# Unread TensorE products placed where three stages of a graph network kernel meet

## The chip, the cores and the metric

The kernel runs on one core of a Trainium2 chip. It is one launch with three stages that follow each other. The metric is the device time of the launch in microseconds; lower is better. TensorE's clock has two levels, 1.2 and 2.4 GHz; the profile lists the granted clock as a share of the full one, so 0.50 is the lower level.

## The reference, cut to what matters

There are 128 graphs of 128 nodes with 512 features each. An attention layer with 16 heads and a bias from the adjacency matrix is followed by a residual and a layer norm; then each graph is sent to one of four experts, multiplied by that expert's weights and its adjacency, batch-normalised over all graphs of the same expert, and added and layer-normalised again.

```python
# attention, per graph: x is 128x512, adj 128x128
a = einsum('bhnd,bhmd->bhnm', q, k) * scale + (adj + adj)[:, None]
p = softmax(a)                       # rows that are all zero give 0
x = layernorm(x + einsum('bhnm,bhmd->bhnd', p, v) @ Wo.T)
# experts
top1 = argmax(x.mean(axis=1) @ router_w + router_b)
out  = adj @ (x @ expert_w[top1])
# batch norm over all graphs of one expert: sums of out and out*out per expert
mean, var = s / cnt, ss / cnt - mean * mean
x = layernorm(x + relu((out - mean[top1]) * rsqrt(var[top1] + eps) * gamma[top1] + beta[top1]))
```

## The kernel before, in words

**Attention stage.** It works on one graph per step, 128 steps, four unrolled; the last four steps (124 to 127) are written out behind the loop. Weights and activations are split into a high and a low part, and each product is made of three passes (high by high, high by low, low by high). In step t TensorE transposes the 16 heads' probabilities (four groups, `transposes(c)`, line 235), multiplies them by the values (`weighted_values`, L243), computes the scores of graph t+1 (`scores`, L197), values of graph t+2 (`v_parts`, L185) and four query or key units of graph t+3 (`qk_unit`, L176), and the output product of graph t (L293). The softmax of t+1 runs meanwhile: VectorE adds the bias and finds the maxima (L384), ScalarE takes exponentials (L316), GpSimd scales by the row sums (L519). VectorE and ScalarE copy the transposed probabilities out of PSUM (L434, L344). In the last three steps the work for later graphs is missing, so step 126 has no values or units to compute, and step 127 no scores either. VectorE adds the residual and normalises (L461 to L494), SyncE stores the result. A semaphore `qk_done[1]` counts the copies (VectorE) of the units that lie in the PSUM bank `BANK_A`.

**Expert stage.** All engines meet at the end of a stage. Then GpSimd clears the accumulators (L819, L820), ScalarE and VectorE split the four experts' weights into high and low parts (L720, L787), of which two are loaded in this stage, and TensorE computes `y = adj @ x` of the first two graphs (`y_product`, L658, f32 operands) and the router scores (L664). It then waits for the last weight split (`e_lo_done`) and enters the loop: per graph one `y_product` two graphs ahead and the product with the chosen expert's weights (`out_product`, L680). ScalarE copies it out and squares it, GpSimd adds both to the sums of the expert (L830, L834).

**Last stage.** TensorE sums the accumulators over the rows (L944, 16 instructions), transposes the sums (L950); VectorE and GpSimd compute mean, variance and the reciprocal root (L1018 to L1035, L1093); TensorE transposes the result (L954) and spreads it into rows (L964, L970), VectorE and ScalarE copy these (L1042, L1133). Then a loop over 128 tiles in a ring of 16: GpSimd multiplies a tile (L1104), TensorE adds the shift (L984, L985), VectorE adds the residual and takes statistics (L1053, L1058), GpSimd takes the reciprocal root for each four tiles (L1119), ScalarE normalises and stores. The loads of a tile wait for the ring slot's store.

Each engine takes its instructions in the order written; what ties them is semaphores.

Of the kernel before, what the change touches and what calls it, by code (L numbers as in the profile page):

```python
# [25 lines left out]
P = 128  # L26
# [18 lines left out]
def attention_phase(nc, io, W_hi, W_lo, w_stage, expert_w_in, ident, x1_dram, B, D):  # L45
    C = D // P
# [6 lines left out]
    Q, K, V, O = range(4)  # L53

    with ExitStack() as ctx:
# [32 lines left out]
        bank = [ctx.enter_context(nc.psum_tensor(f"att_bank{i}", [P, D], F32)) for i in range(8)]  # L88
# [24 lines left out]
        def for_steps(eng, body):  # L113

            with eng.Fori(0, LAST // UNROLL) as i:
                for s in range(UNROLL):
                    body(i * UNROLL + s, s, i, False)
            for s in range(UNROLL):
                body(LAST + s, s, LAST // UNROLL, True)
# [49 lines left out]
        @block.tensor  # L169
        def _(pe):  # L170
            def qk_unit(n, c, which, par, b):

                dst = bank[b][:, 0:GN]
                todo = [(w, x, k) for w, x in passes(W_hi, W_lo, xt_hi, xt_lo) for k in range(C)]
                for m, (w, x, k) in enumerate(todo):
                    mm = pe.matmul(dst, w[:, which, k, c * P:(c + 1) * P], x[:, par, k, :],  # L176
                                   start=m == 0, stop=m == len(todo) - 1)
                mm.then_inc(qk_ps, 1)

            def v_parts(s, b):  # L180

                par, j = (s // 2) % 2, s % 2
                todo = [(x, w, k) for x, w in passes(xt_hi, xt_lo, W_hi, W_lo) for k in range(C)]
                for m, (x, w, k) in enumerate(todo):
                    mm = pe.matmul(bank[b][:, :], x[:, par, k, j * P:(j + 1) * P], w[:, V, k, :],  # L185
                                   start=m == 0, stop=m == len(todo) - 1)
                    if m == len(todo) - 1:
                        mm.then_inc(v_ps, 1)
                    yield

            def scores(s):

                par, j = (s // 2) % 2, s % 2
                for c in range(C):
                    for r in range(HC):
                        rows = slice(r * HD, (r + 1) * HD)
                        mm = pe.matmul(bank[r][:, c * P:(c + 1) * P],  # L197
                                       qk[rows, par, Q, c, j * P:(j + 1) * P],
                                       qk[rows, par, K, c, j * P:(j + 1) * P], start=True, stop=True)
                mm.then_inc(s_ps, 1)  # L200

            for n in range(8):
                if n == 0:
                    pe.wait_ge(xt_lo_done, 1)
                if n % C == 0:
                    pe.wait_ge(w_lo_done, n // C + 1)
                if n >= 2:
                    pe.wait_ge(qk_done[n % 2], n // 2)  # L210
                qk_unit(n, n % C, n // C, 0, BANK_B - n % 2)
            for done in qk_done:
                pe.wait_ge(done, 4)
            scores(0)
            pe.wait_ge(w_lo_done, 3)
            for s in range(2):
                for _ in v_parts(s, BANK_B - s):
                    pass
            pe.wait_ge(xt_lo_done, 2)
            for n in range(8, AHEAD):  # L220
                if n < 10:
                    pe.wait_ge(v_done, n - 7)
                else:
                    pe.wait_ge(qk_done[n % 2], n // 2)
                qk_unit(n, n % C, Q, 1, BANK_B - n % 2)
            pe.wait_ge(const_done, 3)

            def body(t, s, i, last):


                def transposes(c):
                    pe.wait_ge(probs_done, 4 * t + c + 1)
                    for r in range(HC):
                        h = c * HC + r
                        mm = pe.transpose(bank[c][:, r * P:(r + 1) * P], probs[:, h * P:(h + 1) * P],  # L235
                                          ident[:, :])
                    mm.then_inc(pt_ps, 1)

                def weighted_values(c):
                    pe.wait_ge(pt_odd if c % 2 else pt_even, 2 * t + c // 2 + 1)  # L240
                    for r in range(HC):
                        h = c * HC + r
                        mm = pe.matmul(bank[BANK_O][r * HD:(r + 1) * HD, c * P:(c + 1) * P],  # L243
                                       v_sb[:, s, h * HD:(h + 1) * HD], probs_t[:, h * P:(h + 1) * P],
                                       start=True, stop=True)
                    if c == C - 1:
                        mm.then_inc(pv_ps, 1)

                def some_values(n):
                    for _ in range(n):  # L250
                        next(values, None)

                if exists(t, last, 2):
                    pe.wait_ge(res_done, t + 1)
                    values = v_parts((s + 2) % UNROLL, BANK_WO)
                else:
                    values = iter(())
                pe.wait_ge(v_done, t + 1)
                transposes(0)
                transposes(1)  # L260
                transposes(2)
                transposes(3)
                some_values(6)
                for c in range(C):
                    weighted_values(c)
                if exists(t, last, 1):


                    for done in qk_done:
                        pe.wait_ge(done, 2 * (t + 1 - (s + 1) % 2) + 4)  # L270
                    scores((s + 1) % UNROLL)
                some_values(6)

                def next_unit(k):

                    ahead = s + 3
                    if k == 0 and s % 2:
                        pe.wait_ge(xt_lo_done, i * 2 + ahead // 2 + 1)
                    pe.wait_ge(qk_done[k % 2], AHEAD // 2 + 2 * t + k // 2)
                    qk_unit(AHEAD + 4 * t + k, k, ahead % 2, (ahead // 2) % 2, BANK_B - k % 2)  # L280

                more_units = exists(t, last, 3)
                if more_units:
                    next_unit(0)
                pe.wait_ge(w_lo_done, 4)
                pe.wait_ge(o_lo_done, t + 1)
                if exists(t, last, 2):
                    pe.wait_ge(v_done, t + 3)
                else:
                    pe.wait_ge(res_done, t + 1)  # L290
                todo = [(a, w, k) for a, w in passes(o_hi, o_lo, W_hi, W_lo) for k in range(C)]
                for m, (a, w, k) in enumerate(todo):
                    mm = pe.matmul(bank[BANK_WO][:, :], a[:, k, :], w[:, O, k, :],  # L293
                                   start=m == 0, stop=m == len(todo) - 1)
                mm.then_inc(wo_ps, 1)
                if more_units:
                    for k in range(1, UNITS):
                        next_unit(k)

            for_steps(pe, body)  # L300

        @block.scalar
        def _(act):
# [237 lines left out]
def expert_phase(nc, io, W_hi, W_lo, w_stage, expert_w_in, ones, expert_row, kept, out_sum, out_sq,  # L541
# [4 lines left out]
    C = D // P  # L546
    HALF = C // 2
    ROUNDS = 2
    with ExitStack() as ctx:
# [51 lines left out]
        def for_steps(eng, body):  # L601


            def rounds(i, last):
                for n in range(ROUNDS):
                    for s in range(UNROLL):
                        r = i * ROUNDS + n
                        body(r * UNROLL + s, s, r, last, (n, s) == (ROUNDS - 1, UNROLL - 1))

            with eng.Fori(0, B // (ROUNDS * UNROLL) - 1) as i:  # L610
                rounds(i, False)
            rounds(B // (ROUNDS * UNROLL) - 1, True)
# [36 lines left out]
        def _(pe):  # L649
# [11 lines left out]
            def router_scores(pair):  # L661
                pe.wait_ge(part_done, 2 * pair + 2)
                pe.wait_ge(expert_done, pair + 1)
                pe.matmul(ps_scores[:, :, :].rearrange("p g e -> p (g e)"), ones[:, :],  # L664
                          part_score[:, :, :].rearrange("p g e -> p (g e)"),
                          start=True, stop=True).then_inc(scores_ps, 1)
# [19 lines left out]
            for s in range(2):  # L686
                y_product(s, s, 0)
            router_scores(0)
            pe.wait_ge(e_lo_done, E)

            loaded = []
# [16 lines left out]
                    loaded.append(load_expert(t + 1))  # L708

            for_steps(pe, body)  # L710

        @block.scalar
        def _(act):
# [125 lines left out]
def norm_phase(nc, io, ident, ones, expert_row, kept, out_sum, out_sq, x1_dram, y_dram, out_dram, B, D, E):  # L839

    C = D // P
# [6 lines left out]
    with ExitStack() as ctx:  # L848
# [89 lines left out]
        def _(pe):  # L938
# [10 lines left out]
            for c in range(C):  # L949
                mm = pe.transpose(ps_cols[:, c, :], sums_sb[:, c * P:(c + 1) * P], ident[0:2 * E, 0:2 * E])  # L950
            mm.then_inc(cols_ps, 1)

            pe.wait_ge(cols_done, 1)
            pe.transpose(ps_col_t, cols[:, :, :, :].rearrange("p a w n -> p (a w n)"),  # L954
# [262 lines left out]
```

## Time and profile before

| | |
|---|---|
| median of 3 runs | 2780.07 us (2777.33 to 2781.09) |
| the profiled execution's own time | 2777.71 us |
| its span, first to last instruction | 2776.0 us |
| mean granted TensorE clock | 0.985 |
| busy share PE, DVE, ACT, POOL | 96%, 69%, 54%, 46% |
| instructions | 77841 |

The span is the time between the first and the last instruction on any engine; the execution's time is a little longer. PE is TensorE, PEld its weight loads, DVE VectorE, ACT ScalarE, POOL GpSimd, SP SyncE. Busy shares are averages over three stages with different limits. The attention stage lasts until 1997 us, the expert stage until 2514.7 us, the last stage to the end. A row of a timeline gives the start, the duration, the engine, the line of the kernel, the operation, what it writes and reads, how many instructions were merged into the row, and in brackets how long the engine was idle before it and what ended that. Ends of products are modelled and include a tail in which the next one already runs.

### The profile page before, as it was taken

Reading aid. Unit: us, or ns where it says so; the run is one execution under the profiler, and the core shown is the slowest. Engines: PE = TensorE matmul, PEld = TensorE weight load, DVE = VectorE, ACT = ScalarE, POOL = GpSimd, SP = SyncE. Lnnn points to the kernel's source line nnn. Section 1 sums busy time; section 2 is a strip of 40 time slices with the busy share of each in tenths; the row PEclk is TensorE's granted clock in tenths of the full one; section 3 lists DMA queues with packets and bytes.
Section 4 is the critical chain, followed back from the end, with each engine's and each line's share of the span. In section 5 each row is a group of like instructions: output and inputs, shape, how many; then the busy total and the mean of one; then the engine's idle time right before and its main releaser. Section 6 shows DMA issues by size and latency. Waiting matters only on the chain. (4 is left out here: it accounts for less than half of the span.)

```text
span 2776.0 us, 77841 instructions
## 1 busy us (share of the span) xinstructions
PE 2660.1 (96%) x22583; PEld 2264.4 (82%) x22584; DVE 1921.5 (69%) x8351; ACT 1511.9 (54%) x5391; POOL 1282.4 (46%) x1174
## 2 busy tenths in 40 slices
PE   8999999999999999999999999999699999997776
PEld 7898989898888888898989898888588888883322
DVE  6777777777777777777777777777633333335887
ACT  5566665656565656565656656565534444442444
POOL 2343434333433343333334343333256666666887
PEclk9999999999999999999999999999799999998998
DMA  3111111111111111111111111111234444445999
GB/s 147 62 53 54 53 61 53 54 57 57 58 49 64 51 57 53 61 53 54 53 61 53 54 53 61 55 52 57 70 120 137 133 137 132 136 134 198 398 405 346
DMA packets 169427, 277.32 MB, mean 100 GB/s; under 512 B 19378, under 2 KB 52146, under 8 KB 168882
## 3 DMA queue, kind: packets, MB, share of 16 engines
q1 hardware_dynamic: 150962, 243.36, 26.2%
q10 hardware_dynamic: 18432, 33.56, 3.2%
q8 instruction: 15, 0.25, 0.0%
q14 instruction: 18, 0.15, 0.0%
HBM read 184.57 MB, written 92.27 MB: 100 GB/s over the span
## 5 line engine op out<-in xcount | busy, mean ns | idle before, releaser
L519 POOL TENSOR_TENSOR probs<-probs,row_scale 128x512 f32<-128x512 f32 x512 | 532.6, 1040 | 1107.6 <-DVE row_scale L408 1104.7
L316 ACT ACTIVATE probs<-neg_s,neg_max 128x128 f32<-128x128 f32 x2048 | 793.3, 392 | 138.1 <-DVE neg_max L384 138.1
L384 DVE CUSTOM_DVE_ANT_0 neg_s<-att_bank,adj_nat 128x128 f32<-128x128 f32 x2048 | 442.6, 286 | 3.8 <-PE att_bank L197 1.7
L316 ACT ACTIVATION_READ_ACCUMULATOR probs<-neg_s,neg_max 128x1 f32 x2048 | 390.6, 191 | 0.0
L393 DVE TENSOR_REDUCE abs_max<-neg_s 128x4 f32<-128x512 f32 x512 | 349.3, 682 | 0.1
L176 PE MATMUL att_bank<-xt_hi,att_w_hi 128*128 128x256 f32 x2048 | 329.3, 283 | 10.9 <-DVE att_w_lo L366 10.9
L176 PE MATMUL att_bank<-xt_hi,att_w_lo 128*128 128x256 f32 x2048 | 329.7, 283 | 0.0
L176 PE MATMUL att_bank<-xt_lo,att_w_hi 128*128 128x256 f32 x2048 | 329.1, 283 | 0.0
L176 PEld LDWEIGHTS att_bank<-xt_hi,att_w_hi 128*128 128x128 f32 x2048 | 298.8, 191 | 30.4 <-issue 10.5
L344 ACT ACTIVATE probs_t<-att_bank 128x512 f32<-128x512 f32 x256 | 152.9, 597 | 283.4 <-PE att_bank L235 283.3
L176 PEld LDWEIGHTS att_bank<-xt_hi,att_w_lo 128*128 128x128 f32 x2048 | 282.7, 191 | 0.0
L176 PEld LDWEIGHTS att_bank<-xt_lo,att_w_hi 128*128 128x128 f32 x2048 | 282.5, 191 | 0.0
L448 DVE TENSOR_TENSOR o_lo<-att_bank,o_hi 128x512 fp32r<-128x512 f32 x128 | 88.5, 692 | 252.8 <-ACT o_hi L347 252.8
L235 PE MATMUL att_bank<-ident,probs 128*128 128x128 f32 x2048 | 248.0, 274 | 6.5 <-POOL probs L519 6.5
L434 DVE COPY probs_t<-att_bank 128x512 f32<-128x512 f32 x256 | 176.0, 687 | 94.9 <-PE att_bank L235 94.9
L235 PEld LDWEIGHTS att_bank<-ident,probs 128*128 128x128 f32 x2048 | 227.8, 141 | 9.2 <-POOL probs L519 5.4
L512 POOL TENSOR_TENSOR xt_lo<-xt_stage,xt_hi 128x1024 fp32r<-128x1024 f32 x64 | 151.4, 2366 | 126.8 <-DVE xt_hi L446 117.1
L347 ACT ACTIVATE o_hi<-att_bank 128x512 fp32r<-128x512 f32 x128 | 76.5, 597 | 234.1 <-PE att_bank L243 234.1
L984 PE MATMUL ps_z<-n_y,ident 128*128 128x512 f32 x256 | 151.6, 676 | 53.4 <-POOL n_y L1104 49.5
L830 POOL TENSOR_TENSOR out_sum<-out_sum,g_out 128x512 f32 x96 | 123.9, 1290 | 141.8 <-ACT g_out L739 141.8
L1139 ACT ACTIVATE n_x<-n_x,n_nb,n_rstd 128x512 f32<-128x512 f32 x128 | 104.2, 814 | 132.3 <-POOL n_nb L1121 80.0
L751 DVE TENSOR_TENSOR products<-ps_y,router_w 128x16 f32<-128x16 f32 x128 | 22.9, 179 | 218.8 <-PE ps_y L658 218.7
(133 smaller groups left out, 5265.5 us busy)
## 6 DMA issues: line engine op xcount, KB each, us to landing
xt_stage<-in_x_t SPq DMA_DIRECT2D x64, 512.0 KB, 3.4
x_nat<-in_x SPq DMA_DIRECT2D x128, 256.0 KB, 2.6
x_scratch<-x SPq DMA_DIRECT2D x128, 256.0 KB, 2.0
g_x<-x_scratch SPq DMA_DIRECT2D x128, 256.0 KB, 2.8
n_x<-x_scratch SPq DMA_DIRECT2D x128, 256.0 KB, 7.5
out_x<-n_x ACTq DMA_DIRECT2D x128, 256.0 KB, 5.5
y_scratch<-g_out SPq DMA_DIRECT2D x96, 256.0 KB, 2.0
n_y<-y_scratch SPq DMA_DIRECT2D x96, 256.0 KB, 5.7
```

What stands on the lines that cost most here:

```text
L176: mm = pe.matmul(dst, w[:, which, k, c * P:(c + 1) * P], x[:, par, k, :], start=m == 0, stop=m == len(todo) - 1)
L235: mm = pe.transpose(bank[c][:, r * P:(r + 1) * P], probs[:, h * P:(h + 1) * P], ident[:, :])
L316: nc.scalar.activation(probs[:, h * P:(h + 1) * P], neg_s[:, h * P:(h + 1) * P], ACT.Exp, bias=neg_max[:, h:h + 1], scale=-1.0, accum_out= ...
L344: nc.scalar.activation(probs_t[:, c * D:(c + 1) * D], bank[c][:, :], ACT.Copy).then_inc(pt_odd, 1)
L384: nc.vector.tensor_tensor_reduce(neg_s[:, h * P:(h + 1) * P], bank[r][:, c * P:(c + 1) * P], adj_nat[:, s], -2.0, BIG, ALU.add, ALU.min, n ...
L393: nc.vector.tensor_reduce(abs_max[:, heads], neg_s[:, c * D:(c + 1) * D].rearrange("p (h m) -> p h m", h=HC), AX_X, ALU.max, apply_absolut ...
L434: nc.vector.tensor_copy(probs_t[:, c * D:(c + 1) * D], bank[c][:, :]).then_inc(pt_even, 1)
L512: nc.gpsimd.tensor_tensor(xt_lo[:, p], xt_stage[:, p], xt_hi[:, p].bitcast(F32), ALU.subtract).then_inc(xt_lo_done, 1)
L519: nc.gpsimd.tensor_tensor(part, part, by, ALU.mult).then_inc(probs_done, 1)
L830: nc.gpsimd.tensor_tensor(acc, acc, src, ALU.add).then_inc(sum_done, 1)
L984: pe.matmul(dst, ident[:, :], y[:, s], start=True, stop=False)
L1139: nc.scalar.activation(x1[:, s], x1[:, s], ACT.Identity, bias=nb[:, u, k:k + 1], scale=rstd[:, u, k:k + 1]).then_inc(out_done, 1)
```

## The change

TensorE runs a fixed number of products whose results nobody reads. They write to PSUM banks that are free at that place. In the attention stage the two last steps get 7, 3, 3 and 2 of them ahead of the four groups of transposes, behind a new wait for the last copy out of `BANK_A`; the last step gets 5 more ahead of its output product, and 32 follow behind the last step. These are 512 columns wide, on the split weights. In the expert stage 32 products of 128 columns on a matrix of ones in f32 stand between the first router scores and the wait for the last weight split, and 14 of 512 columns behind the loop. In the last stage 18 products of 128 columns on the identity stand between the transposes of the sums and the wait for the batch norm columns. Nothing else is changed.

```diff
+            def spin(n):
+                for m in range(n):
+                    pe.matmul(bank[BANK_A][:, :], W_hi[:, O, 0, 0:P], W_hi[:, O, 0, :],
+                              start=True, stop=True)
...
-                transposes(0)
-                transposes(1)
-                transposes(2)
-                transposes(3)
+                chain_bound = last and t >= B - 2
+                if chain_bound:
+                    pe.wait_ge(qk_done[1], 2 * B)
+                for c in range(C):
+                    if chain_bound:
+                        spin((7, 3, 3, 2)[c])
+                    transposes(c)
...
                 pe.wait_ge(w_lo_done, 4)
+                if last and t == B - 1:
+                    spin(5)
                 pe.wait_ge(o_lo_done, t + 1)
...
             for_steps(pe, body)
+            spin(32)
...
             router_scores(0)
+            for m in range(32):
+                pe.matmul(ps_o[0][:, 0:P], ones[:, :], ones[:, :], start=True, stop=True)
             pe.wait_ge(e_lo_done, E)
...
             for_steps(pe, body)
+            for m in range(14):
+                pe.matmul(ps_y[0][:, 0, :], W_hi[:, 0, 0, 0:P], W_hi[:, 0, 0, :], start=True, stop=True)
...
             mm.then_inc(cols_ps, 1)
+            for m in range(18):
+                pe.matmul(ps_z[0][:, 0:P], ident[:, :], ident[:, :], start=True, stop=True)
 
             pe.wait_ge(cols_done, 1)
```

## Rows read from the trace of the kernel before

**Rows 1.** The page: TensorE's granted clock and transfer share in 40 slices, tenths.
```profile
PEclk9999999999999999999999999999799999998998
DMA  3111111111111111111111111111234444445999
```
**Rows 2.** Windows: length, busy us per engine (count), granted clock, transfer share, GB/s.
```profile
1977.40:1980.10 2.70, 0.02 (x1) 0.06 (x1) 2.65 (x12) 2.70 (x15) 1.04 (x1) 1.00 0.00 0
1980.10:1986.90 6.80, 5.95 (x48) 4.18 (x48) 4.54 (x13) 2.17 (x8) 3.62 (x4) 0.50 0.10 39
1991.60:1997.20 5.60, 0.01 (x1) 0.00 (x0) 2.27 (x5) 0.00 (x0) 0.55 (x1) 0.69 0.13 48
2014.55:2017.92 3.37, 3.37 (x12) 3.06 (x13) 0.76 (x3) 0.60 (x1) 0.00 (x0) 0.54 0.02 5
2515.14:2523.88 8.74, 8.74 (x17) 1.62 (x17) 5.83 (x8) 0.00 (x0) 2.66 (x6) 0.80 0.81 258
2530.95:2536.60 5.65, 5.34 (x32) 5.16 (x32) 2.77 (x4) 2.04 (x4) 0.00 (x0) 0.50 1.05 384
2538.76:2545.22 6.46, 6.46 (x12) 3.20 (x13) 2.49 (x4) 0.00 (x0) 6.46 (x6) 0.65 0.12 42
```
**Rows 3.** Timeline, attention: two full steps, then the last two steps.
```profile
1926.68 1.08 PE L243 MATMUL att_bank<-probs_t,v_sb 128*32 128x128 f32 x32
...
1938.78 1.91 PE L235 MATMUL att_bank<-ident,probs 128*128 128x128 f32 x16
...
1980.08 1.07 PE L235 MATMUL att_bank<-ident,probs 128*128 128x128 f32 x4 [2.70 <-POOL probs L519]
...
1985.17 0.68 DVE L434 COPY probs_t<-att_bank 128x512 f32<-128x512 f32 x1
1985.27 1.87 PE L243 MATMUL att_bank<-probs_t,v_sb 128*32 128x128 f32 x32
...
1990.55 1.07 PE L293 MATMUL att_bank<-att_w_hi,o_lo 128*128 128x512 f32 x4
```
**Rows 4.** The meeting of the engines between attention and expert stage: durations ns, start.
```profile
L55 PEldq DRAIN  x1: 2967/2967/2967, 1988.7 to 1988.7; - x1
...
1997.29 0.10 POOL L812 MEMSET scores<- 1x16 f32 x1 [3.19 <-POOLq L55]
```
**Rows 5.** Timeline, head of the expert stage, then one step of its loop.
```profile
2001.44 3.81 PE L658 MATMUL ps_y<-adj_t,g_x 128*128 128x129 f32 x16 [9.83 <-POOL out_sq L820]
...
2011.66 2.29 DVE L787 TENSOR_TENSOR exp_w_lo<-kept,exp_w_hi 128x2048 fp32r<-128x2048 f32 x1 [0.64 <-ACT exp_w_hi L720]
2014.55 2.08 PE L658 MATMUL ps_y<-adj_t,g_x 128*128 128x129 f32 x8 [8.24 <-DVE exp_w_lo L787]
...
2105.23 1.05 PE L658 MATMUL ps_y<-adj_t,g_x 128*128 128x129 f32 x8
2106.04 1.18 PE L680 MATMUL ps_o<-exp_w_hi,y_hi 128*128 x4
```
**Rows 6.** Timeline, end of the expert stage and the batch norm chain.
```profile
2510.04 1.09 PE L680 MATMUL ps_o<-exp_w_hi,y_lo 128*128 x4
...
2513.16 1.26 POOL L834 TENSOR_TENSOR out_sq<-out_sq,g_sq 128x512 f32 x1
...
2515.14 5.30 PE L944 MATMUL ps_sums<-out_sum,sum_into 128*8 128x512 f32 x8 [4.00 <-POOL sum_into L1080]
...
2529.76 0.42 PE L954 MATMUL ps_rows<-ident,bn_cols 128*64 128x128 f32 x1 [4.80 <-DVE bn_cols L1035]
...
2535.91 0.69 DVE L1042 COPY mul_row<-ps_rows 128x512 f32<-128x512 f32 x1 [0.59 <-PE ps_rows L964]
```
**Rows 7.** Timeline, the last loop: GpSimd's first reciprocal root, two waits of TensorE.
```profile
2548.57 1.01 POOL L1119 TENSOR_TENSOR n_rstd<-n_ve,half_u 128x4 f32<-128x4 f32 x1 [1.35 <-DVE n_ve L1071]
...
2601.17 1.95 PE L984 MATMUL ps_z<-n_y,ident 128*128 128x512 f32 x2 [2.21 <-POOL n_y L1104]
...
2629.21 1.12 PE L984 MATMUL ps_z<-n_y,ident 128*128 128x512 f32 x2 [2.15 <-POOL n_y L1104]
```

## The prediction

> **What bounds the kernel now.** I read the forty slices first. TensorE's granted clock is full almost everywhere and dips most in slice 29 (1943 to 2012 us) and in slice 37 (2498 to 2568 us), where the three stages meet [rows 1]. The change puts all its products there; the other slices matter only as a place where time can be given back. The windows show what stands ahead of a dip. From 1977.4 to 1980.1 us TensorE is idle at a clock of 1.00, the next stretch is granted 0.50 (the lower of the two levels, 1.2 against 2.4 GHz) although TensorE is busy for 5.95 of its 6.80 us; after 1991.6 it is idle again and the mean of 0.69 over 5.6 us means that the clock fell some 2.1 us in. The first work of the expert stage (0.54), the sums of the batch norm chain (0.80 over 8.74 us), its row products (0.50) and the first sums of the last loop (0.65) all run wholly or partly at the lower level [rows 2]. The timeline tells what that costs: sixteen transposes take 1.91 us at full clock, four take 1.07 us at half; 32 weighted-value products take 1.08 and 1.87 us [rows 3].
>
> Who waits for TensorE there? In the last two attention steps no next graph fills in, so each burst of products stands in the chain softmax, transposes, weighted values, output product. At the head of the expert stage the weight split sets the first product: VectorE's last split starts at 2011.66 and lasts 2.29 us, and TensorE, idle for 8.24 us, starts at 2014.55 [rows 5]. From there the expert loop is TensorE's own. In the batch norm chain the sums and the row products stand on the path [rows 2, 6].
>
> **Part one, the last two attention steps.** The added wait on the odd copies holds nothing: the copies it asks for are issued in step 124, two steps back. Queued behind it are the transposes. Products of 512 columns start every 0.23 us (the last four output products take 1.07 us with a tail of 0.15 us [rows 3]). In step 126 the 7 products (1.6 us) delay the first transposes by about 1 us, but VectorE comes to copy these later still; the 3, 3 and 2 fill gaps. With the clock kept, the last transposes and the weighted values run at full speed, and late next is VectorE's copy of the transposed probabilities. By the same reckoning as below, step 126 gives 0.7 us at its weighted values and 0.9 us at the scores, so all of step 127's softmax starts 0.9 us earlier. In step 127 the copy of 1985.17 moves to 1984.27 and ends 0.68 us later, and half of the weighted values (0.5 us) and their tail follow it: done at 1985.57 instead of 1987.14 (1985.27 + 1.87), **1.57 us** gained [rows 3]. The 5 products ahead of the output product (1.15 us) lie in its wait. Bounds: 0.5 us (only the last transposes and weighted values double) and 1.7 us; I take 1.57, as no row of this chain then needs the lower clock.
>
> Then 32 products stand ahead of the end of the stage, which ends for all engines together. Now TensorE's drain is over at 1991.7, and the next stage starts at 1997.29, after the last normalisation and its store [rows 4]. Without the products that would become 1995.72. With them: the last output product is issued by 1991.46 - 1.57 = 1989.89, 32 x 0.23 = 7.3 us later it is 1997.2, and with a tail of 0.15 and 0.2 us of handover 1997.5 (my estimate; GpSimd's end at 2514.42 to TensorE's next work at 2515.14 bounds it at 0.7 [rows 6]). The cover is overrun by 1.8 us, and the expert stage starts **0.2 us later** (bounds: 0.3 earlier at 0.215 us per product, 1.3 later with the small gain).
>
> The Trainium skill, page "TensorE: Matmul & The Clock Gate", Part 4, says that transposes don't count as busy for the clock gate and that the full clock does not engage for them. The trace differs: the sixteen at 1.91 us ran at twice the speed of the four at 1.07 us [rows 3]. By the page's rule the transposes would stay slow and about 0.5 us of the 1.57 would go; I go by the row.
>
> **Part two, the expert head.** TensorE is idle from about 1997.4 until the zeroing of the accumulators lets it start (2001.44 now, 2001.64 then), 4.2 us, and 2.7 us of idleness has been enough for half clock [rows 2, 3, 5]. So the first y products run slow as now, and so do the first of the 32 products of 128 columns. Each of these is two instructions. At full clock eight such start within 0.81 us (2105.23 to 2106.04), 0.101 us each; at half clock eight take 2.08 instead of 1.05 us, so 0.20 us each by twice the pace and 0.24 us by the 3.81 us of the first sixteen; I take 0.215 us [rows 5]. All 64 cost 6.5 us fast and 13.8 us slow. The room is the 8.24 us from 2006.31 to 2014.55. [...] With 4.7 us slow, 22 instructions are slow and 42 fast: 4.7 + 4.3 = 9.0 us, 0.75 us too long. Against that the stretch from 2014.55 to 2017.92 holds 0.54 x 3.37 = 1.8 us of work at full clock: 1.5 us back. I take a net gain of 1.2 us, between 0.75 and the 1.5 of an earlier rise; bounds 0.3 lost (the 6.4 us case) and 1.5. Over both parts 1.2 - 0.2 = **1.0 us**, and the TensorE-bound loop carries it on.
>
> **Part three, the batch norm chain.** The 14 products after the expert loop take 14 x 0.23 = 3.2 us from 2510.95 (2510.04 + 0.91), to 2514.3 with their tail; GpSimd's last sum ends at 2514.42 [rows 6]. Hidden, by 0.1 us; without that cover 0.2 us. TensorE then waits under a microsecond in place of 4.00, so the sums run at full clock: (1 - 0.80) x 8.74 = **1.7 us** [rows 2], all on the path.
>
> The 18 products on the identity take 36 x 0.101 = 3.6 us in a wait of 4.80 us [rows 6]: hidden with 1.1 us to spare; slow, 36 x 0.2 = 7.2 us, 2.4 us late. After them come 2.3 us with almost nothing on TensorE: the 1.1 us and the 1.2 us from 2529.76 to 2530.95. If the clock holds, the row products are no longer last: VectorE copies four rows of 0.69 us, the last of which waited 0.59 us for its products [rows 6], and the 5.65 us [rows 2] become 0.6 + 4 x 0.7 = 3.4: 2.25 us less. If not, nothing. In the final loop one wait of 2.15 us kept the clock, one of 2.21 us lost it [rows 7]; the single product in between speaks for keeping, so I take three quarters, **1.7 us** (bounds 0 and 2.25). Before the last loop TensorE waits some 2.5 us again, so its first sums will likely be slow as now; if fast, the reciprocal root at 2548.57, which waited 1.35 us for the statistics [rows 7], comes 1.3 us earlier. I take **0.4 us** (bounds 0 and 1.3).
>
> Does the last loop keep it? While the first sums run, the transfer share is 0.12 [rows 2]: the ring is filled and waits for the first normalised tiles. The bulk of the transfers starts with these, so the end moves with them.
>
> **Sum.** 1.0 + 1.7 + 1.7 + 0.4 = 4.8 us off the profiled execution's 2777.71 (span 2776.0 and 1.7 around it): 2772.9 us. That execution lies 2.4 us below the median of the runs; from 2780.07 the same sum gives **2775.3 us**.
>
> **Rivals.** (a) *The clock is kept throughout.* Head 1.5, start 0.3 earlier, then 1.7, 2.25 and 1.3: 7 us, 2773.0 us. For it: the products lie in the idle times ahead of each dip. Against: two waits of over 2 us stay empty. (b) *The last loop gives it back*, its transfers setting the end whatever starts them: only the 1.0 us and perhaps half a microsecond are left, 2778.5 us. For it: a transfer share of nine tenths in the last slices [rows 1]; against: the 0.12 at the loop's start. (c) *Unread products at half clock stand in the way.* TensorE takes its queue in order, so a real product waits for all put ahead of it. If these products don't raise or hold the clock, the 32 of 512 columns take 14 us and start the expert stage 6.6 us late, the 64 instructions there overrun by 5.6 us and the 36 by 2.4: 15 us slower, 2795 us. It decides once the head is over 3.8 us late, which is what the chain gives; all 64 slow would do that even with 1.5 us back (5.6 - 1.5 = 4.1). Against it: a stretch of y and expert products brought the clock up in 3.1 us [rows 2]. (d) *The clock doesn't answer but everything fits*: 2780 us.
>
> **How the numbers follow.** 0.2%, 5.6 us, is about what a measurement of this kernel can tell from no change. The forecast, 2.5 to 5.5 us gained (2774.6 to 2777.6): 0.50; (a) 0.32; (b) with (d) 0.11; (c) 0.07. The range takes in a head that loses 0.3 us, row products from 0 to 2.25 us, (a), and (b): 2771.0 to 2780.0 us, with a little below (a) for the spread of the runs (2777.3 to 2781.1). Faster by over 0.2%: 0.33, nearly all of it (a); within: 0.60; slower: 0.07.
>
> **What would show it.** Four transposes of the last step within 0.65 us; the expert stage starting between 1997.0 and 1998.6; the first products with expert weights at a clock of 1.00; the sums done in 7.0 us; the last mul_row copies 0.7 us apart. I'm wrong if the clock is 0.50 in step 127, if the first product after the split starts over 2 us later after it than now, or if the last loop lasts longer by what the chain gave.

## The result and the profile after

The changed kernel takes 2773.82 us, the median of ten executions (2772.14 to 2774.94); ten of the kernel before on the same chip have a median of 2779.38 us (2777.33 to 2783.92). The ratio is 0.9979, with a 95% interval of 0.9971 to 0.9988: some 5.6 us or 0.2% faster. The prediction was 2775.3 us, a gain of 4.8 us; the 5.6 us lie just above the 2.5 to 5.5 us to which it gave its largest chance, on the side of rival (a). The profiled executions are 2772.14 against 2777.71 us, each 1.7 us below the median of its own ten, so the two traces can be set against each other.

The page of the changed kernel, TensorE's granted clock in 40 slices: the dip of slice 29 [rows 1] is gone and that of slice 37 too at this resolution.

```profile
PEclk9999999999999999999999999999999999999998
```

The next fence gives windows of the changed kernel (start and end, length, busy time and count on PE, PEld, DVE, ACT and POOL, granted clock, transfer share, GB/s). The first two are the times of the first two of [rows 2], then come the head of the expert stage, the sums, the 18 products on the identity, the row products and the first products of the last loop.

```profile
1977.40:1980.10 2.70, 1.90 (x11) 1.32 (x10) 2.63 (x12) 2.70 (x15) 1.05 (x2) 1.00 0.00 0
1980.10:1986.90 6.80, 5.93 (x58) 3.82 (x57) 4.28 (x12) 2.45 (x7) 3.62 (x4) 1.00 0.11 41
1990.56:1998.23 7.67, 7.42 (x33) 5.82 (x31) 2.27 (x5) 0.00 (x0) 0.55 (x1) 1.00 0.09 35
2001.90:2005.20 3.30, 2.82 (x13) 2.82 (x14) 3.06 (x4) 0.43 (x2) 0.43 (x1) 0.50 0.95 271
2006.73:2014.12 7.39, 7.39 (x66) 7.20 (x65) 5.97 (x11) 3.96 (x3) 0.00 (x0) 1.00 0.73 261
2514.38:2521.42 7.04, 7.04 (x17) 1.43 (x17) 5.83 (x8) 0.00 (x0) 2.66 (x6) 1.00 0.81 242
2522.43:2526.72 4.29, 4.28 (x38) 4.09 (x36) 0.80 (x5) 0.00 (x0) 2.92 (x1) 1.00 1.03 394
2526.72:2530.70 3.98, 2.63 (x28) 2.48 (x28) 2.40 (x7) 1.50 (x4) 0.00 (x0) 1.00 1.05 388
2533.95:2541.00 7.05, 7.05 (x15) 3.53 (x15) 3.40 (x6) 0.00 (x0) 7.05 (x6) 0.73 0.43 152
```

Before, the stretch from 1980.10 was granted 0.50, the sums 0.80 and the row products 0.50 [rows 2]; all three now have 1.00. What the products did not keep stands there too: the first work of the expert stage still ran at 0.50 until about 2005.2, and the last loop began at the lower clock.

The timeline of the changed kernel has the same places in the order of time (start, duration, engine, line, operation, what it writes and reads, count, idle time before it and what ended that).

```profile
1983.95 0.66 PE L241 MATMUL att_bank<-ident,probs 128*128 128x128 f32 x4
...
1989.65 1.07 PE L304 MATMUL att_bank<-att_w_hi,o_lo 128*128 128x512 f32 x4
1990.56 7.41 PE L231 MATMUL att_bank<-att_w_hi 128*128 128x512 f32 x32
...
1998.23 0.10 POOL L828 MEMSET scores<- 1x16 f32 x1 [5.02 <-POOLq L55]
...
2002.38 3.42 PE L670 MATMUL ps_y<-adj_t,g_x 128*128 128x129 f32 x16 [4.41 <-POOL out_sq L836]
...
2006.73 7.39 PE L702 MATMUL ps_o<-ones 128*128 128x128 f32 x64
...
2012.02 2.29 DVE L803 TENSOR_TENSOR exp_w_lo<-kept,exp_w_hi 128x2048 fp32r<-128x2048 f32 x1 [0.33 <-ACT exp_w_hi L736]
...
2014.77 1.15 PE L670 MATMUL ps_y<-adj_t,g_x 128*128 128x129 f32 x8 [0.64 <-DVE exp_w_lo L803]
...
2017.16 1.10 PE L692 MATMUL ps_o<-exp_w_lo,y_hi 128*128 x4
...
2510.16 3.37 PE L726 MATMUL ps_y<-exp_w_hi 128*128 128x512 f32 x14
2514.38 3.60 PE L960 MATMUL ps_sums<-out_sum,sum_into 128*8 128x512 f32 x8 [0.84 <-POOL sum_into L1098]
...
2529.72 1.38 DVE L1060 COPY mul_row<-ps_z 128x512 f32<-128x512 f32 x2
2531.11 0.69 DVE L1060 COPY mul_row<-ps_rows 128x512 f32<-128x512 f32 x1
...
2532.56 2.48 POOL L1122 TENSOR_TENSOR n_y<-n_y,mul_row 128x512 f32<-128x512 f32 x2 [6.08 <-DVE mul_row L1060]
2533.95 2.07 PE L1002 MATMUL ps_z<-n_y,ident 128*128 128x512 f32 x2 [2.46 <-POOL n_y L1122]
...
2543.44 1.01 POOL L1137 TENSOR_TENSOR n_rstd<-n_ve,half_u 128x4 f32<-128x4 f32 x1 [1.01 <-DVE n_ve L1089]
```

The last output products, the last transposes, the sums (3.60 us in the place of 5.30 [rows 6]) and the row copies (0.69 us apart, none waiting) are at full clock. The 32 products end at 1997.97, and the expert stage starts 0.26 us after that: they now set its start. At the expert head TensorE finished its unread products at 2014.12, just ahead of the split (2014.31), and then went on at full clock; before, the same eight y products took 2.08 us [rows 5].

Where the 5.6 us came from, read as the start of the same work in either trace:

| work | before | after | earlier by | predicted |
|---|---|---|---|---|
| last output products of step 125 | 1963.91 | 1964.47 | -0.56 | 0 |
| first instruction of the expert stage | 1997.29 | 1998.23 | -0.94 | -0.2 |
| second expert pass (L692) of the first graph | 2017.92 | 2017.16 | 0.76 | 1.0 |
| sums | 2515.14 | 2514.38 | 0.76 | 1.0 |
| first n_y of the last loop | 2537.36 | 2532.56 | 4.80 | 4.4 |
| first reciprocal root | 2548.57 | 2543.44 | 5.13 | 4.8 |
| end of the span | 2776.0 | 2770.4 | 5.6 | 4.8 |

Two of these steps are chance, and they cancel: the 0.56 us arose before any changed instruction, and the last weights came 0.58 us earlier within the expert stage (the last split ends 16.08 us after the stage's start, 16.66 before; in the other traces below 15.4 to 17.6, whatever the edit). What is left between these two traces is -0.38 us at the start of the expert stage, 1.12 at its head, 1.70 in the sums, 2.34 in the rest of the chain, 0.33 before the first reciprocal root and some 0.4 in the last loop.

The trace of before is one of several that differ in the same places. In the traces below without the attention products, it takes 26.86 to 27.43 us from the last output products of step 125 to those of step 127, where before has 26.64, and 33.61 to 34.26 us to the expert stage, where before has 33.38. In those without the 14 products the sums take 8.36 to 9.53 us, where before has 8.74. So the first and the third of these terms are differences of two single traces; against most other traces without the products they would come out more favourable to the change.

### The profile page after: what moved, and what is told of

Read it like the earlier page. It is cut to its first block and busy times, and to the rows that moved or that the text cites. A ratio compares the mean times of both kernels' runs of the same rounds, so it can differ in the third digit from the quotient of the medians.

```text
span 2770.4 us, 78203 instructions
## 1 busy us (share of the span) xinstructions
PE 2681.7 (97%) x22764; PEld 2283.2 (82%) x22765; DVE 1922.2 (69%) x8351; ACT 1511.9 (55%) x5391; POOL 1282.0 (46%) x1174
```

## The experiments

The theory: each group of products pays by the clock alone, at its own place, and costs what it holds up in TensorE's queue. Against it stood that the products as such (not their clock) help, that one place carries all of the gain, and that the last loop takes gains back. Every run was timed against the kernel before on the same chip; the medians of before were 2779.98 (first four kernels), 2779.76 (the next four) and 2780.18 us (the last three). An interval is about 2.5 us wide on either side, so a single part of 1 to 2 us is told by its trace and only the larger ones by the times.

### The attention products alone

```diff
-            for m in range(32):   # on ones
+            for m in range(0):
...
-            for m in range(14):
+            for m in range(0):
...
-            for m in range(18):
+            for m in range(0):
```

> Only the products of the attention stage stay (7, 3, 3, 2, 5 and the 32 behind the loop); the expert head and the batch norm chain are as before the change. Theory (the gain is half-clock stretches removed, and a product ahead of the stage's end costs its own time): the output product of the last step ends some 1.5 us earlier, the 32 products give all of it back, the expert stage starts 0.2 to 0.5 us later than before; the head starts at half clock as before. Result 0.2 to 0.5 us slower than before, ratio 1.000. Rival (warming the engine ahead of the expert stage helps the head by itself): the stretch from the last weight split to the end of the first expert product is at full clock, 1.4 us back, about 1 us faster than before.

2779.86 us, ratio 0.9998 (0.9989 to 1.0008): nothing. The trace tells why. From the last output products of step 125 to those of step 127 it takes 25.19 us (26.64 before, 25.18 in the changed kernel), so the 1.46 us are there; to the first instruction of the expert stage it takes 33.78 us (33.38 before). The gain is real and the 32 products behind it use it up. The expert head is as before (second pass 4.03 us after the split, 3.97 before), so nothing shows a head that is helped by itself.

### The products on ones alone

```diff
-                chain_bound = last and t >= B - 2
+                chain_bound = False
...
-                    spin(5)
...
-            spin(32)
...
-            for m in range(14):
+            for m in range(0):
...
-            for m in range(18):
+            for m in range(0):
```

> Only the 32 products on ones in the expert head. Theory: they end before or within 1 us after the last weight split, the first y product and expert product after it run at 1.00 instead of 0.54, the loop starts 0.7 to 1.4 us earlier than before and the time falls by as much, 2778.2 us against 2779.4. Rival (they need the 32 products of the attention tail ahead of them to be warm in time): they run at half clock for over 6 us, end 1.5 us or more after the split, and the loop starts no earlier than before.

2778.57 us, ratio 0.9996 (0.9987 to 1.0006): not told from nothing. In the trace the rival of the expectation came true in its outcome: the products end 3.1 us behind the split, and the loop starts no earlier. The clock was still low when the products began, and the timeline and a window of this run show them in the way:

```profile
2007.53 9.60 PE L699 MATMUL ps_o<-ones 128*128 128x128 f32 x64
2016.97 1.06 PE L667 MATMUL ps_y<-adj_t,g_x 128*128 128x129 f32 x8
```

```profile
2007.53:2017.13 9.60, 9.60 (x67) 9.60 (x68) 6.01 (x11) 3.63 (x2) 0.00 (x0) 0.76 0.42 147
```

The split ended at 2014.07, TensorE came to its y product 2.9 us later. The second expert pass starts 4.72 us after the split; before it was 3.97, in the changed kernel 2.85 us. So this is rival (c) of the prediction in one execution: the product after the split came 2.3 us later behind it than before (2.9 against 0.6 us).

### The products of the batch norm chain alone

```diff
-                chain_bound = last and t >= B - 2
+                chain_bound = False
...
-                    spin(5)
...
-            spin(32)
...
-            for m in range(32):   # on ones
+            for m in range(0):
```

> Only the 14 products behind the expert loop and the 18 in the batch norm chain. Theory: the sums take 7.0 us in place of 8.7, the row products stop being last (2.2 us), so the first GpSimd product of the last loop starts 4 us earlier relative to the end of the expert loop, and the time falls by 4 to 5 us: 2775 us. Rival (the last loop is paced by its transfers and gives it back): the chain is 4 us shorter and the last loop longer by 2 us or more, 2777.5 us.

2777.49 us, ratio 0.9989 (0.998 to 0.9999): 2.5 us faster, about half of what was expected. From the sums' start to the first n_y it takes 19.61 us (22.22 before, 18.18 in the profile of the changed kernel). The sums gave their 1.70 us; the clock then fell in the middle of the row products, so that these gave only 0.9.

### Without the 32 products at the end of the attention stage

```diff
-            spin(32)
```

> The changed kernel without the 32 products behind the attention loop. Theory: these only hold up the stage's end; without them the expert stage starts 1.8 us earlier. The clock is down before the y products in either kernel (4.4 us of waiting with them), so the 32 products on ones still fit the wait for the weight split (7.4 us of 8 with them), unless their slow part grows from 1.9 to over 3 us. Time 1.2 to 1.8 us below the changed kernel, 2772.3 us. Rival (they are what lets the clock rise in time in the head): the products on ones overrun the split by 1.5 us or more and eat the gain: 2773.8 us or more.

2772.74 us, ratio 0.9972 (0.9963 to 0.9982). With the 32 products it is 2773.82 us and 0.9979 (0.9971 to 0.9988): the intervals overlap, so the times don't separate the two. By the trace the expert stage starts 32.04 us after the mark in step 125, 1.72 us earlier than with the 32 products. But TensorE then waited 9.93 us for its first work, and the products on ones took 9.17 us, so that the product behind them started 1.7 us after the split:

```profile
1997.01 0.10 POOL L827 MEMSET scores<- 1x16 f32 x1 [3.29 <-POOLq L55]
...
2001.16 3.81 PE L669 MATMUL ps_y<-adj_t,g_x 128*128 128x129 f32 x16 [9.93 <-POOL out_sq L835]
...
2005.89 9.17 PE L701 MATMUL ps_o<-ones 128*128 128x128 f32 x64
2014.90 1.06 PE L669 MATMUL ps_y<-adj_t,g_x 128*128 128x129 f32 x8
```

The second pass starts 3.52 us after the split, 2.85 in the changed kernel: 0.7 of the 1.7 us are given back.

### Twice the products on ones

```diff
-            for m in range(32):   # on ones
+            for m in range(64):
```

> The changed kernel with 64 products on ones in the expert head in place of 32. Theory (TensorE takes its queue in order): 64 more instructions of 0.115 us, 7.4 us, of which 0.6 us of waiting cover a part: the first product after the weight split starts 6.8 us later and the time is 6.5 to 7 us above the changed kernel, 2780.5 us. Rival (products nobody reads are passed by the ones that wait): 2774 us.

2780.37 us, ratio 1.0002 (0.9993 to 1.0011): the gain is gone, 6.5 us above the changed kernel. The timeline shows the queue's order:

```profile
2006.83 16.71 PE L702 MATMUL ps_o<-ones 128*128 128x128 f32 x128
2023.38 1.06 PE L670 MATMUL ps_y<-adj_t,g_x 128*128 128x129 f32 x8
```

The split ended at 2014.48; the product that waited for it came 8.9 us later, 8.4 us more than in the changed kernel. The granted clock was 0.70 up to the split (2006.83 to 2014.50) and 1.00 behind it (to 2023.40). A queue that is too long loses at full clock as well, so it is the room that decides, as in rival (c).

### The same products, 8 columns wide

```diff
-                    pe.matmul(bank[BANK_A][:, :], W_hi[:, O, 0, 0:P], W_hi[:, O, 0, :],
+                    pe.matmul(bank[BANK_A][:, 0:8], W_hi[:, O, 0, 0:P], W_hi[:, O, 0, 0:8],
...
-                pe.matmul(ps_o[0][:, 0:P], ones[:, :], ones[:, :], start=True, stop=True)
+                pe.matmul(ps_o[0][:, 0:8], ones[:, :], ones[:, 0:8], start=True, stop=True)
```

and so for the 14 and the 18.

> The changed kernel with as many products in the same places, each 8 columns wide. Theory (the array has to work for the clock to stay): products this narrow do not hold it, the sums and row products run at half clock as before, the time is 2779 to 2780.5 us; the expert stage starts 1 us earlier at most. Rival (the instructions as such help, by keeping TensorE's queue and its instruction supply going): 2774 us as in the changed kernel.

2786.0 us, ratio 1.0019 (1.0009 to 1.0028): slower than the kernel before. So products as such, in this number and at these places, do nothing good. The timeline and three windows of this run:

```profile
2008.01 11.67 PE L702 MATMUL ps_o<-ones 128*128 128x8 f32 x64
...
2019.53 1.85 PE L670 MATMUL ps_y<-adj_t,g_x 128*128 128x129 f32 x7
...
2520.78 6.06 PE L960 MATMUL ps_sums<-out_sum,sum_into 128*8 128x512 f32 x8 [2.55 <-POOL sum_into L1098]
```

```profile
2005.00:2010.00 5.00, 4.51 (x32) 4.32 (x32) 3.52 (x14) 2.02 (x3) 0.00 (x0) 0.81 0.99 326
2010.00:2015.00 5.00, 5.00 (x27) 5.00 (x27) 3.46 (x4) 2.99 (x2) 0.00 (x0) 0.54 0.76 268
2015.00:2020.00 5.00, 5.00 (x24) 5.00 (x25) 1.38 (x1) 0.00 (x0) 0.00 (x0) 0.50 0.00 0
```

The narrow ones began at full clock: from 2008.01 to 2010.00 it was 1.00, and 20 instructions ran in these 2 us. Then it fell to the lower level while TensorE is shown busy for 10 of 10 us, and 24 instructions took 5.00 us, 0.21 us each, as long as wide ones at half clock. In the changed kernel the wide ones stood in the same place at 1.00 throughout. The product behind the narrow ones started 3.1 us after the split (2016.38): the queue cost of rival (c) without its return. The batch norm chain lost too. Its 36 narrow instructions took 6.69 us in a wait that was 4.80 us before [rows 6], and from the sums to the first n_y it takes 24.64 us (22.22 before). At the attention steps and ahead of the sums the narrow ones also fill less of the wait than wide ones do (2.55 us stay idle ahead of the sums, 0.84 in the changed kernel), so the head alone tells width from filling.

### Attention and expert head together

```diff
-            for m in range(14):
+            for m in range(0):
...
-            for m in range(18):
+            for m in range(0):
```

> The products of the attention stage and the 32 on ones together, none in the batch norm chain. Alone these two parts gave 0.1 and 1.4 us. Theory (the two parts help each other: with the 32 behind the attention loop the clock falls later, so its slow stretch ends earlier in the head and the products on ones end before the weight split instead of 2.3 us behind it): 2.5 to 3.5 us gained, 2776.8 us. Rival (the parts add up, and what the whole change has beyond their sum lies in the chain): 1.5 us gained, 2778.4 us.

2777.39 us, ratio 0.999 (0.9981 to 0.9999): 2.8 us faster, where the two alone make 1.5 by their medians. In the trace the products on ones took 7.39 us and ended 1.4 us ahead of the split:

```profile
2003.28 3.53 PE L670 MATMUL ps_y<-adj_t,g_x 128*128 128x129 f32 x16 [4.41 <-POOL out_sq L836]
...
2007.61 7.39 PE L702 MATMUL ps_o<-ones 128*128 128x128 f32 x64
2016.80 1.15 PE L670 MATMUL ps_y<-adj_t,g_x 128*128 128x129 f32 x8 [1.80 <-DVE exp_w_lo L803]
```

The idle time ahead of the y products is 4.41 us here and was 9.84 us in the run with the products on ones alone. That the attention products help the head through this shorter wait is what the two traces suggest, but it isn't shown: the difference of 1.3 us lies inside the intervals, and the second trace of the changed kernel (below) has the same short wait with slow products behind it.

### The 14 products before the sums alone

```diff
-                chain_bound = last and t >= B - 2
+                chain_bound = False
...
-            spin(32)
...
-            for m in range(32):   # on ones
+            for m in range(0):
...
-            for m in range(18):
+            for m in range(0):
```

> Only the 14 products behind the expert loop. Theory: the sums take 7.0 us in place of 8.7, 1.7 us gained, 2778.2 us; the row products stay at half clock. Rival (the 14 overrun GpSimd's last sum and give part of it back): the next stage starts 0.5 us or more later against the end of the expert loop, 1 us gained or less.

2777.77 us, ratio 0.9993 (0.9984 to 1.0002): by the times alone unclear. In the trace the sums take 7.04 us and the stretch to the first n_y 20.53 us, 1.69 us less than before; the row products ran at half clock as before (the first four in 1.08 us).

### The changed kernel once more

No edit.

> The changed kernel once more, for a second trace. Theory (where a wait of two microseconds stays empty, the clock is kept in some executions and lost in others): the head of the expert stage or the row products stand otherwise in this trace than in the first, and the times spread by 2 to 3 us around 2773.8. Rival (the first trace is what always happens): full clock in the row products until 2530 us again, and the same clock at the first y products.

2775.0 us, ratio 0.998 (0.9971 to 0.999): the same as the first time. Its trace is not the same. Lines of its timeline and a window:

```profile
2007.09 9.66 PE L702 MATMUL ps_o<-ones 128*128 128x128 f32 x64
...
2530.96 0.62 PE L988 MATMUL ps_z<-bn_col_t,add_from 64*64 64x128 f32 x4
2531.39 1.05 PE L982 MATMUL ps_z<-bn_col_t,mul_from 64*128 64x128 f32 x4
```

```profile
2007.09:2016.59 9.50, 9.50 (x65) 9.50 (x66) 6.13 (x11) 3.82 (x2) 0.00 (x0) 0.75 0.55 198
```

The products on ones took 9.66 us: the granted clock was 0.51 from 2007 to 2012 and 1.00 behind that. In the row products it fell again, so that the chain took 19.52 us where the first trace has 18.18. The late weights of this execution (split end at 2015.84) hid the former: second pass 2.83 us after the split.

### The chain with its waits filled

```diff
-            for m in range(18):
+            for m in range(20):
...
+            for m in range(3):     # behind the transposed columns
+                pe.matmul(ps_z[0][:, 0:P], ident[:, :], ident[:, :], start=True, stop=True)
...
+            for m in range(7):     # ahead of the last loop, behind its waits
+                pe.matmul(ps_rows[0][:, 0:P], ident[:, :], ident[:, :], start=True, stop=True)
```

on the kernel with the chain's products alone.

> The run with the batch norm chain's products alone (14 and 18; 2777.5 us), with 20, 3 and 7 as in the filled kernel. Theory: its gain of 2.5 us fell short of 4 to 5 because the clock went in the wait of 2.3 us ahead of the row products; closed, the row products take 0.7 us per expert and the time is 2774.5 to 2775.5 us. Rival (the last loop gives it back): the chain is 2 us shorter and the time stays at 2777.5.

2775.41 us, ratio 0.998 (0.9971 to 0.999): 4.3 us faster. That is some 2 us better than the chain's products alone, though the intervals of the two overlap. From the sums to n_y 18.17 us; the rows ran at full clock throughout. Windows of the rows and of the seven last products:

```profile
2531.69:2534.61 2.92, 2.92 (x32) 2.78 (x32) 2.25 (x4) 1.77 (x3) 0.00 (x0) 1.00 1.05 389
2535.38:2538.10 2.72, 2.72 (x15) 2.72 (x16) 0.00 (x0) 0.00 (x0) 2.24 (x2) 0.62 1.06 389
```

The seven came 0.77 us after the rows and still lost the clock in this execution: it was 1.00 in the first 0.62 us of them and 0.50 to 0.52 in the next 2 us.

### All waits filled

The changed kernel with the three edits above, 22 instead of 32 products at the end of the attention stage, and 14 on the identity at the start of the expert stage, which need nothing of that stage:

```diff
-            spin(32)
+            spin(22)
...
+            for m in range(14):    # first in the expert stage, ahead of its first wait
+                pe.matmul(ps_o[0][:, 0:P], ident[:, :], ident[:, :], start=True, stop=True)
             pe.wait_ge(filled, 5)
```

> The changed kernel with its open waits closed: 22 products in place of 32 behind the attention loop, 14 of 128 columns on the identity at the very start of the expert stage, 20 in place of 18 in the batch norm chain, 3 more behind the transposed columns and 7 ahead of the last loop. Theory (what is left of the loss is half clock after waits that stay empty, and the overrun of the 32): the expert stage starts 1.5 us earlier than in the changed kernel, its head is at full clock, the row products always run fast (in the two runs with the chain's products so far one lost the clock there, which costs up to 2.2 us) and the first sums of the last loop too (1 us): 2769.5 to 2771 us, against 2773.8 of the changed kernel. Rival (the products only move the loss: each of them stands ahead of a real product): no better than 2772.7.

2769.82 us, ratio 0.9965 (0.9952 to 0.9979), 9.9 us faster than before and the fastest of all; its five executions (2769.19 to 2771.92) lie below all twenty of the changed kernel, whose ratios' intervals it overlaps. Timeline and windows:

```profile
1989.86 5.15 PE L231 MATMUL att_bank<-att_w_hi 128*128 128x512 f32 x22
...
1999.87 2.05 PE L670 MATMUL ps_y<-adj_t,g_x 128*128 128x129 f32 x16 [0.75 <-POOL out_sq L838]
...
2541.00 1.01 POOL L1143 TENSOR_TENSOR n_rstd<-n_ve,half_u 128x4 f32<-128x4 f32 x1 [0.18 <-DVE n_ve L1095]
```

```profile
1999.87:2001.92 2.05, 2.05 (x16) 1.86 (x16) 2.05 (x2) 0.00 (x0) 0.00 (x0) 1.00 0.73 174
2004.19:2011.58 7.39, 7.39 (x66) 7.20 (x65) 5.08 (x11) 3.95 (x3) 0.00 (x0) 1.00 0.77 277
2532.35:2540.00 7.65, 7.65 (x19) 3.19 (x20) 5.54 (x13) 0.00 (x0) 7.65 (x7) 1.00 0.53 195
```

The expert stage starts 31.94 us after the mark in step 125 (33.76 in the changed kernel), the clock is full at every place where before it dipped, and GpSimd's first reciprocal root waits 0.18 us instead of 1.01: there GpSimd is the bound now, and TensorE's clock has little left to give. The times tell only the five edits together. In the trace, against before, 1.44 us lie at the start of the expert stage, 1.12 at its head, 4.05 in the chain and 1.16 before the first reciprocal root, 7.8 us in all.

## Why the prediction was right, step by step

The mechanism, a clock kept up so that work on the path runs at full speed, was the predicted one at the last attention steps, the sums and the row products. The head came out by luck, and so did part of the total, which was too small by 0.8 us (0.4 by the second ten executions).

**Attention.** Predicted gain 1.57 us, measured 1.46; in all six other traces with these products it is 25.17 to 25.22 us between the marks against 26.64 before and up to 27.43 in other traces without them. Each four transposes of the last step took 0.66 us at full clock where they had 1.07 [rows 3] to 1.12. The 32 products took 7.41 us as worked out, and their overrun made the expert stage start 0.38 us later than in the one trace of before (predicted 0.2); without them it started 1.34 us earlier than before.

**Expert head.** Predicted 1.2 us net, measured 1.12, but not as the prediction saw it, and the agreement is luck. It let the products run slow for 4.7 us and end 0.75 us late. No row of before gives these 4.7 us, nor the 6.4 us of its lower bound. In the profiled execution the clock was back before the products began and they ended 0.2 us early; where it was still low, the slow stretch was 3.7, 4.6 and 4.75 us (0.80 over 9.17, 0.76 over 9.60, 0.75 over 9.50 us). These slow cases (9.17, 9.60 and 9.66 us against the predicted 9.0) cost what the arrival of the last weights left uncovered: 0.7 us against the best case in one, 1.9 us in another, nothing in the third. Two terms were mis-sized. The early rise was to give 1.5 us and gave 1.12: with the products out of the way in time, the stretch from the first y product to the second expert pass takes 2.39 us, not 1.8. It took 1.8 to 2.1 us only behind an overrun. And the price at full clock is 0.116 us each (64 in 7.39 us), not 0.101; the loop's y products [rows 5] were too short a row for it. For the same reason the 18 products on the identity took 4.29 us, not 3.6, and left 0.58 us of their wait.

**Sums.** 1.70 us, as predicted. They take 7.04 us in every trace with the 14 products at full width; what that gains depends on the trace without them, 1.3 to 2.5 us.

**Row products.** Predicted three quarters of 2.25 us. It is not a fixed share: 2.3 us in the profiled execution, and 1.0, 0.9, 0.7 and 0.7 in the four other traces of the same chain (19.52, 19.61, 19.84 and 19.84 us against 22.22, less the sums' 1.70), a mean of 1.1. The profiled execution was the best of them. The time of the fall differs between executions. The prediction took two waits of the last loop as the two ends; the share that it read from them was too large for a typical execution.

**Last loop.** The first sums stayed slow (0.73, and 0.65 before) and gave 0.33 us of the 0.4; fully filled they give 1.2 (10.05 us from the first n_y to the root, 11.21 before). From the first root to the end it takes 226.3 to 228.5 us in all thirteen traces, 227.4 before: it neither gives back what came ahead (rival b) nor does it add to it; the last 0.4 us of the profiled execution are in this spread.

**Rivals.** (a), 7 us, was not reached because the clock was not kept throughout; the version that keeps it gains 9.9 us by the medians and 7.8 us by its trace in the places of the products, with 10 products fewer ahead of the expert stage. (c) does not happen in the two traces of the changed kernel; it does with 64 products, with narrow ones, and with the 32 on ones alone, where they start at half clock. (d) is refuted by the clock itself.

The Trainium skill, page "TensorE: Matmul & The Clock Gate", Part 1, says of a kernel with waits between bursts that each burst starts at the lower clock, and that the same kernel shows different numbers of slow products from run to run. The traces agree on the second (the head's 64 instructions took 7.39 and 9.66 us in two executions of one kernel). On the first they agree only in part. Behind a wait of 4.41 us the first y products of the changed kernel stood at 0.50. But the sums of the kernel before, behind a wait of 4.00 us [rows 6], began at full clock at 2515.14 and fell to the lower level within a microsecond, while TensorE worked. Two windows of that trace:

```profile
2515.00:2516.00 1.00, 0.86 (x2) 0.19 (x3) 0.97 (x5) 0.00 (x0) 0.87 (x4) 1.00 0.09 8
2516.00:2517.00 1.00, 1.00 (x3) 0.26 (x2) 1.00 (x1) 0.00 (x0) 1.00 (x1) 0.50 0.32 41
```

Of transposes, Part 4 of that page of the Trainium skill says that they don't engage the full clock; the four transposes at 0.66 us with a granted clock of 1.00 differ from it. The rows list them as MATMUL, so they don't tell whether the engine's transpose mode was on.

What stays open: why the clock falls earlier in one execution than in the next, and whether attention and head help each other beyond the spread of the runs.

## What to carry to other kernels

Products nobody reads pay where an engine's wait precedes work that sets the end, and only as far as they fit inside that wait: here 1.70 us for 14 products in a wait of 4.00 us, and a loss of 6.5 us for 32 too many in another. Read such a gain from several traces of either kernel: the part of one place differed by 1.7 us between executions of the same chain. Count what else the queue's end releases, since 32 products ahead of a meeting of all engines used up the 1.46 us that the products before them had gained. Work that needs nothing of the next stage can go behind the meeting instead, where it fills the same wait without delaying anybody.

## What the runs showed of the hardware

- Products of 8 columns, back to back, began at a granted clock of 1.00 and it fell to 0.50 within 2.5 us, while TensorE is shown busy throughout. At 0.50 24 of their instructions took 5.00 us, 0.21 us each, as long as those of 128 columns (13 in the first 2.70 us of the second execution of the changed kernel, at 0.50). At full clock those of 128 columns took 0.116 us (64 in 7.39 us).
- Two traces of one kernel differ in where the clock falls: the 64 instructions on ones took 7.39 and 9.66 us, and the batch norm chain 18.18 and 19.52 us.
- Behind a wait of 0.77 us, after a stretch at full clock, the seven products ahead of the last loop went from 1.00 to half clock in one execution (14 instructions in 2.72 us) and stayed at 1.00 in another (1.80 us).
